# Low parts of h times W2 by seven products of quarter blocks, and PSUM emptied after each half of a tile

## What is computed

```
n  = layernorm(x)
uv = n @ in_proj_w + in_proj_b;  u, v = halves of uv;  v = silu(v)
v  = depthwise conv of 3 taps over time + conv_b
h_t = sigmoid(logit_a) * h_(t-1) + ssm_b * v_t;  y_t = ssm_c * h_t + ssm_d * v_t
a  = layernorm((u * silu(y)) @ out_proj_w + out_proj_b + n) * ln_w + ln_b
x1 = x + layernorm(a)
h  = gelu(layernorm(x1) @ T(W1) + b1)         (512 -> 2048)
x2 = x1 + layernorm(h @ T(W2) + b2)           (2048 -> 512)
```

## Time and profile before

| | us |
|---|---|
| Median of three runs | 1427.58 |
| Lowest and highest of them | 1425.25 and 1428.63 |
| The profiled execution, its own time | 1427.88 |
| Its span, first to last instruction | 1425.9 |
| DVE busy in the span | 1119.8 |
| ACT busy in the span | 911.8 |
| One tile period in the middle | 86.65 |

### The profile page before, as it was taken

One profiled execution on the slowest core, in us unless ns is written; L12 is line 12 of the kernel. 1 busy time (PEld: TensorE's weight loads), 2 busy tenths in 40 slices (PEclk: granted clock), 3 DMA queues, 4 the chain that ended last, 5 costly groups with the idle time before them and its releaser, 6 DMA issues.

```text
span 1425.9 us, 23101 instructions
## 1 busy us (share of the span) xinstructions
PE 1403.4 (98%) x8426; PEld 825.4 (58%) x8426; DVE 1119.8 (79%) x1889; ACT 911.8 (64%) x1504; POOL 414.2 (29%) x522
## 2 busy tenths in 40 slices
PE   6999999999999999999999999999999999999998
PEld 4444556656566564666646566565665646655664
DVE  8999987878779686786868778687786867998744
ACT  7998675657666565675656757476665756753553
POOL 5234241322413232142421413224132321422211
PEclk9999999999999999999999999999999999999999
DMA  8703320311311122111311203113121221001200
GB/s 248 257 27 85 65 78 17 86 30 31 89 30 60 31 53 67 31 60 31 89 31 31 74 17 89 31 30 89 23 67 30 53 67 31 31 1 30 60 30 30
DMA packets 156001, 82.26 MB, mean 58 GB/s; under 512 B 132720, under 2 KB 132720, under 8 KB 155760
## 3 DMA queue, kind: packets, MB, share of 16 engines
q1 hardware_dynamic: 155888, 80.79, 22.4%
HBM read 31.49 MB, written 16.78 MB: 34 GB/s over the span
## 4 chain that ended last, share of the span: by engine, by line
PE 86%; DVE 4%; issue 2%; DMA 0%; ACT 0%; POOL 0%; POOLq 0%; DVEq 0%; ACTq 0%
PE f1b L573 14%; PE f1b L574 14%; PE f2b L597 14%; PE f2b L599 14%; PE misc L538 6%; PE misc L536 6%; PE misc L537 6%; PE misc L550 3%; PE misc L552 3%; PE misc L551 3%; PE f2b L622 1%; PE f2b L621 1%; DVE w L1234 0%; DVE g_lo L949 0%; DMA xs<-x_dram 0%
## 5 line engine op out<-in xcount | busy, mean ns | idle before, releaser
L573 PE MATMUL f1b<-x3T,w 128*128 128x256 f16 x1792 | 397.5, 273 | 0.0
L574 PE MATMUL f1b<-x3T,w 128*128 128x256 f16 x1792 | 397.5, 273 | 0.0
L597 PE MATMUL f2b<-w,ring 128*128 128x512 fp8e5 x960 | 363.9, 379 | 0.8 <-DVE ring L847 0.8
L599 PE MATMUL f2b<-w,ring 128*128 128x512 fp8e5 x960 | 363.8, 379 | 0.0
L1652 ACT ACTIVATE ring<-f1b,par 128x256 f32<-128x256 f32 x480 | 201.2, 471 | 227.0 <-PE f1b L574 226.7
L2088 POOL TENSOR_SCALAR ve<-mv 128x4 f32<-128x4 f32 (+2 forms) x89 | 35.2, 395 | 729.8 <-DVE mv L839 729.7
L847 DVE SCALAR_TENSOR_TENSOR ring<-ring,f_sc 128x512 f16<-128x512 f32 x256 | 200.4, 796 | 30.1 <-ACT ring L1666 30.0
L574 PEld LDWEIGHTS f1b<-x3T,w 128*128 128x128 fp8e5 x1792 | 175.4, 98 | 32.6
L573 PEld LDWEIGHTS f1b<-x3T,w 128*128 128x128 fp8e5 x1792 | 175.3, 98 | 32.5
L1666 ACT ACTIVATE ring<-ring,f_sc 128x512 f16<-128x512 f32 x256 | 182.0, 718 | 0.0
L536 PE MATMUL misc<-x1T,win_hi 128*128 128x512 f16 x456 | 172.8, 379 | 0.0
(11 more groups left out here) (233 smaller groups left out, 2143.4 us busy)
## 6 DMA issues: line engine op xcount, KB each, us to landing
out_dram<-hb SPq DMA_DIRECT2D x64, 256.0 KB, 2.0
xs<-x_dram SPq DMA_DIRECT2D x14, 1024.0 KB, 6.0
ring<-w1t_dram SPq DMA_DIRECT2D x3, 1024.0 KB, 13.5
stage<-w2t_dram SPq DMA_DIRECT2D x3, 1024.0 KB, 8.2
x1T<-tp SPq DMA_TRANSPOSE x68, 3.1
xs<-x_dram SPq DMA_DIRECT2D x4, 256.0 KB, 3.6
stage<-w_in_dram SPq DMA_DIRECT2D x4, 256.0 KB, 5.0
xs<-x_dram SPq DMA_DIRECT2D x2, 512.0 KB, 6.6
```

The costliest lines, as they stand in the source:

```text
L573: pe.matmul(o_, w, src[:, k, h * TH:(h + 1) * TH], start=k == 0, stop=False)
L574: mm = pe.matmul(o_, w, src[:, KC + k, h * TH:(h + 1) * TH], start=False, stop=k == KC - 1)
L597: pe.matmul(f2b[q][:, :], h_hi[:, i % H_SLOTS, qs], w2[:, chunk, :], start=chunk == 0, stop=False)
L599: mm = pe.matmul(f2b[q][:, :], h_lo[:, i % H_SLOTS, qs], w2[:, chunk, :], start=False, stop=chunk == FC - 1)
```

## The change

**Products.** In tiles 2 to 13 (`seven(t)`) a unit's low parts, two blocks of rows by two chunks, meet W2, two chunks by two halves of its 512 columns, as a product of 2 x 2 blocks in Strassen's way: seven products of 256 columns in place of four of 512. Three of them take h_lo as it is (a11, a12, a22) and four take the sums `s1` to `s4`; four take combinations of W2 (`combined`), which DVE makes once, in step 3, in eight operations (`combine`). The high parts stay as they were.

**Sums.** The sums are made by `presums` for two units at once: four DVE operations on 16-bit values, 128 x 2 x 128, placed behind the lo of every odd unit. `presum` and `combined` lie in `stage`.

**PSUM.** The seven products need all four banks f2b in each half of a tile: f2b0 and f2b1 take the high parts and a part of the products, f2b2 and f2b3 quarter sums. So they are emptied twice: `drain(t, h)` is four operations of 256 columns, one sum of two blocks, and two operations of 512 columns. drain(t, 0) stands between the h_adds, drain(t, 1) at the head of the next step in place of the f_adds. The first half's result has a buffer in stage (`hb_first`). f2(t, 8) now waits for drain(t, 0), and PE does it behind f1(12) instead of ahead of o; f2(t, 0) waits for the whole of drain(t - 1, 1).

**Left taps.** From tile 3 on the left taps of tile s stand at the end of step s, behind the last t_lo, rather than in step s + 1.

The diff, cut to its core:

```
+    def seven(t):
+
+        return 1 < t < NT - 2
...
 
+            def f2_seven(t, j):
+
+                i, (h, chunks) = FC * t + j, unit(j)
+                p, r = chunks[0], i % H_SLOTS
+                if p == 0:
+                    pe.wait_ge(f_ok, NB * t + 2 * h)
+                if not seven(t - 1) and j == 0:
+                    pe.wait_ge(comb_ok, 8)
+                pe.wait_ge(hh_ok, i + 1)
+                for q in range(2):
+                    for n, chunk in enumerate(chunks):
+                        pe.matmul(f2b[q][:, :], h_hi[:, r, n * TH + q * P:n * TH + (q + 1) * P], w2[:, chunk, :],
+                                  start=p == 0 and n == 0, stop=False, skip_group_check=True)
+                pe.wait_ge(sums_ok, 4 * rank(i) + 4)
+                a11, a21, a12, a22 = (h_lo[:, r, n * P:(n + 1) * P] for n in range(4))
+                s1, s2, s3, s4 = (presum[:, i % 4, n, :] for n in range(4))
+                t1, t2, t3, t4 = (combined[:, n, p, :] for n in range(4))
+                left, right = slice(0, TH), slice(TH, 2 * TH)
+
+                def product(bank_, cols, a, b, start=False):
+
+                    return pe.matmul(bank_[:, cols], a, b, start=start, stop=p == PAIRS - 1, skip_group_check=True)
+
+                product(f2b[2], left, a11, w2[:, p, left], p == 0)
+                product(f2b[0], left, a12, w2[:, p + PAIRS, left])
+                product(f2b[3], right, s1, t1, p == 0)
+                product(f2b[2], right, s2, t2)
+                product(f2b[3], left, s3, t3)
+                product(f2b[0], right, s4, w2[:, p + PAIRS, right])
+                product(f2b[1], left, a22, t4).then_inc(f2_mm, 1)
+
             def f2(t, j):
+                if seven(t):
+                    f2_seven(t, j)
+                    return
                 i = FC * t + j
                 if j % PAIRS == 0 and t > 0:
-                    pe.wait_ge(f_ok, NB * (t - 1) + 2 + 2 * (j // PAIRS))
+                    pe.wait_ge(f_ok, NB * t if seven(t - 1) else NB * (t - 1) + 2 + 2 * (j // PAIRS))
...
-                left = [lambda j=j: f2(fa, j) for j in range(half(s) - LAG, half(s))] if fa is not None and s < NT else []
+                mid = min(half(s), PAIRS) if seven(fa or 0) else half(s)
+                left = [lambda j=j: f2(fa, j) for j in range(half(s) - LAG, mid)] if fa is not None and s < NT else []
...
-                        if j >= half(s) + LAG:
+                        if j >= mid + LAG:
...
+            def combine(q, g):
...
+                ve_.tensor_tensor(combined[:, q, ps, :], in0, in1, ALU.subtract, saturate=False).then_inc(comb_ok, 1)
...
+            def presums(t, j, last):
+
+                i = FC * t + j
+                r, z, k = i % H_SLOTS, i % 4, 4 * rank(i)
+                a11, a21, a12, a22 = (h_lo[:, r:r + 2, n * P:(n + 1) * P] for n in range(4))
+                s1, s2, s3, s4 = (presum[:, z:z + 2, n, :] for n in range(4))
+                if last:
+                    ve_.wait_ge(sums_ok, k + 3)
+                    ve_.tensor_tensor(s4, a12, s2, ALU.subtract).then_inc(sums_ok, 1)
+                    return
+                ve_.wait_ge(hl_ok, i + 2)
+                ve_.wait_ge(f2_mm, i - 2)
+                ve_.tensor_tensor(s3, a11, a21, ALU.subtract).then_inc(sums_ok, 1)
+                ve_.tensor_tensor(s1, a21, a22, ALU.add).then_inc(sums_ok, 1)
+                ve_.wait_ge(sums_ok, k + 1)
+                ve_.tensor_tensor(s2, a22, s3, ALU.subtract).then_inc(sums_ok, 1)
+
+            def lows(t, js, at):
+
+                items = [(at[j], lambda j=j: lo(t, j)) for j in js]
+                if seven(t):
+                    pairs = [j for j in js if j % 2 == 1]
+                    items += [(at[j] + AT_PRESUM, lambda j=j: presums(t, j - 1, False)) for j in pairs]
+                    items += [(at[j] + AT_PRESUM_LAST, lambda j=j: presums(t, j - 1, True)) for j in pairs]
+                return items
+
+            def drain(t, h):
+
+                dst, k = fo_pair(t, h), 5 * (2 * (t - 2) + h)
+                quarter = dst.rearrange("p j (n c) -> p (j n) c", c=TH)
+                left, right = slice(0, TH), slice(TH, 2 * TH)
+
+                def part(src, cols, out_, in1):
+
+                    ve_.scalar_tensor_tensor(out=out_, in0=src[:, cols], scalar=f_inv[:, 0:1], in1=in1,
+                                             op0=ALU.mult, op1=ALU.add).then_inc(part_ok, 1)
+                def first():
+                    ve_.wait_ge(f2_mm, half_done(t, h))
...
+                    part(f2b[2], left, quarter[:, 0, :], b2_row[:, 0:TH])
+                def second():
+                    part(f2b[3], right, quarter[:, 3, :], b2_step[:, :])
...
+                    part(f2b[2], right, quarter[:, 1, :], quarter[:, 0, :])
...
+                    part(f2b[3], left, quarter[:, 2, :], quarter[:, 1, :])
...
+                    ve_.tensor_tensor(dst[:, :, right], quarter[:, 1:3, :],
...
+                def block_(q):
+                    ve_.wait_ge(part_ok, k + 5)
+                    ve_.scalar_tensor_tensor(out=dst[:, q, :], in0=f2b[q][:, :], scalar=f_inv[:, 0:1], in1=dst[:, q, :],
+                                             op0=ALU.mult, op1=ALU.add).then_inc(f_ok, 1)
+                return [first, second, third, fourth, fifth, lambda: block_(0), lambda: block_(1)]
...
+                if seven(e):
+                    return (spread(AT_F_ADD, .1, drain(e, 1))
...
+                if s < NT - 1:
+                    items += [(at, lambda b=b: taps(s, b, True)) for b, at in enumerate(AT_TAP0_NEXT)]
```

More of the change, by code:

```diff
@@ L346, in hb_of, with fo_pair, fo @@
             return xs[:, NT % X_SLOTS] if c == NT - 1 else hb
+        def fo_pair(t, h):
+            return hb_first if seven(t) and h == 0 else hb[:, 2 * h:2 * h + 2, :]
+        def fo(t, j):
+            return fo_pair(t, j // 2)[:, j % 2, :]
         def xn_of(t, j):
@@ L1559, in _ @@
                     at_lo = AT_LO_PAIR if s == NT else AT_LO
-                    items += [(at_lo[j] if j < len(at_lo) else 1.2 + j, lambda j=j: lo(fa, j))
-                              for j in range(half(s))]
+                    items += lows(fa, range(half(s)), [at_lo[j] if j < len(at_lo) else 1.2 + j for j in range(FC)])
                 run(items)
@@ L1588, in _ @@
                 if c is not None:
+                    parts = drain(fa, 0) if seven(fa) else []
                     for j in range(NB):
                         h_add(c, j)
+                        for part in parts[2 * j:2 * j + 2]:
+                            part()
                         if s == NT - 1:
@@ L2133, in finish @@
                 pool.wait_ge(fn_ok, NB * e + j + 1)
-                pool.tensor_tensor(hb[:, j, :], hb[:, j, :], xs[:, e % X_SLOTS, j, :], ALU.add).then_inc(fin_ok, 1)
+                pool.tensor_tensor(fo(e, j), fo(e, j), xs[:, e % X_SLOTS, j, :], ALU.add).then_inc(fin_ok, 1)
             def keep_state(c, b):
```

74 lines of the change are left out of this document (61 added, 13 removed).

## The result

The changed kernel takes 1503.2 us (median of 4 runs, 1502.8 to 1506.2) against 1426.4 for the kernel before in the same session (1425.1 to 1428.6): a ratio of 1.054, 95% interval 1.052 to 1.056. It is slower by 77 us. The profiled execution took 1506.2 us, with a span of 1504.4.

The account below looks back on a forecast made before the run. PE bound the kernel before; DVE's queue would become the pace. 1427.9 us plus 9 (step 3 to 4), 51 (11 periods at 4.6 more) and 5 (step 15) gave 1493 us, range 1442 to 1532.

Parts of the forecast that it names:

- PE, removed: f2 units on PE: 1.63 us instead of 1.73, extra weight loads free, a period floor of 85.0 us.
- Drain: DVE's emptying of PSUM at the head of a step: 3.8 us, against two f_adds of 1.3 before.
- Sums: DVE's four sums for a pair of units: 1.03 us a pair, 8.2 us a tile (3.1 to 11.8).
- From the drain to gate 1: First stretch of a period: 32.2 us, 2.6 more than before, with PE standing 3.7 us at f2(4).
- From gate 1 to the next drain: Rest of a period: 59.1 us against 57.05 before, PE standing about 1 us at o(2), 0.5 at f2(8).
- The period: One tile, drain to drain: 91.3 us, 4.6 more than before, DVE's queue as the pace.
- The ends: Outside the 11 middle periods: 9 us more from gate 1 of step 3 to step 4's, 5 us in step 15.
- Sums at the plain rate: Rival on DVE's sums: each pair costs 0.44 us more, 1530 us in all; chance 0.2.
- PE as the pace: Rival: DVE's extra work fits its slack and PE stays the pace, 1411 us; chance 0.08.
- The falling clock: Rival: PE's clock falls because PE stops twice a step, 7 us more a step, about 1550 us; chance 0.03.
- DVE's share: Sign in the changed kernel's profile: DVE busy near 88% of the span.
- It can't fit: Step on DVE's room: 12.9 us more work a tile against 8.4 us of true slack and 1.6 us less period.

Follow-up runs that it names:

- e1: Changed kernel without the sums on DVE, the four products reading low parts instead (part of the W2 product left out): 1429.6 us, ratio 1.003.
- e13: e12 with the sums of units 6 and 7 behind gates 0 and 1 in steps 4 to 14: 1411.8 us, ratio 0.991.
- e11: Changed kernel with POOL's four additions of x1 cut to 8 of 512 columns in tiles 2 to 13: 1497.1 us, ratio 1.049.
- e3: Changed kernel with the left conv taps back in the next step, behind the drain: 1542.5 us, ratio 1.082.
- e6: Changed kernel with each drain cut to two operations of 512 columns, quarter sums not added in: 1502.0 us, ratio 1.054.
- e2: Changed kernel with the sums made, but no product reading or waiting for them: 1474.5 us, ratio 1.035.
- e5: Kernel before the change, with the sums of tiles 2 to 13 made on DVE and read by nobody: 1461.3 us, ratio 1.025.
- e7: Changed kernel with lo(4), lo(5) and their sums before the third scan, and lo(10), lo(11), lo(13) with sums in the norms' waits: 1464.9 us, ratio 1.028.
- e9: e7 with drain(t, 0) spread between x1's low parts, h_add(0) sooner, three W2 combinations in waits of step 3: 1447.9 us, ratio 1.016.
- e10: e9 with sums (2, 3) and lo(9) sooner, W2 combinations spread, seven products in tiles 2 to 12 only, old kernel end: 1429.4 us, ratio 1.0024.
- e12: e10 with right taps of blocks 0 and 1 ahead of the drain and lo(8) behind the gates, steps 4 to 14: 1422.0 us, ratio 0.9974.

## Why the prediction was right, and where it was not

The prediction of 1493 us was right in sign and near in size; the likeliest case was the one that came. The path of the prediction, DVE's queue as the pace and PE idle for about 6 us of a period, was right too: PE is idle for 92.10 - 86.11 = 6.0 us. DVE's added work is 12.5 us a tile, 12.9 predicted.

- **PE, removed.** Right: a unit takes 1.63 us, and the weight loads cost nothing. The floor of 85.0 us was 85.24 (PE's busy time) in e1 and 85.21 in e13.
- **Drain.** 3.8 us predicted, 635.56 - 631.69 = 3.87 measured.
- **Sums.** I took 1.03 us a pair. Each sum lasts 0.28 us and starts 0.2 after the one ahead; the four take 0.94. One wait of 0.11 that I had forgotten, of the first sum for the low part just ahead, makes it 1.05. That the two agree to 0.02 us is luck: the sums were taken too slow and a wait was missing. The Trainium skill (VectorE: DVE Perf Modes, "The perf-mode tier table") gives tensor_tensor twice the plain rate for bf16 in SBUF; with the 0.15 us that one element costs, (0.285 - 0.15) / 256 is 0.53 ns an element of fp16, half of the 1.04 of the earlier trace rows. So fp16 behaves here as the table has it for bf16.
- **From the drain to gate 1.** 32.2 us predicted, 33.35 measured. I put PE's one stop of 3.7 us at f2(4). It was 1.88 at f2(2) and 2.31 at f2(4), 4.2 in all. The misplaced term is POOL's blocks: I kept their cost as before, "since DVE's operations there are two-input ones as before". They cost as much as before, but fell on three of the four sums that f2(2) waits for (e11 shows that this stop is theirs). DVE's queue was also longer than I had added up: the sums of units 4 and 5 were ready 27.1 us after the drain's start, not 26.2. Of the 0.9 us 0.41 are idle time ahead of the fourth scan, which starts when ACT has ended its operation ahead of it, and ACT came to that late because of PE's f1 behind the stop at f2(2), as the waits and the order of its queue have it:

```profile
652.31 0.84 ACT L1826 ACTIVATE ring<-f1b,par 128x256 f32<-128x256 f32 x2 [1.36 <-PE f1b L600]
653.04 0.72 ACT L1840 ACTIVATE ring<-ring,f_sc 128x512 f16<-128x512 f32 x1
653.65 0.71 ACT L1875 ACTIVATE yb<-vl,par 128x512 f32<-128x512 f32 x1
...
654.45 1.28 DVE L1071 TENSOR_TENSOR_SCAN vl<-a_par,carry,vl 128x512 f32<-128x512 f32 x1 [0.41 <-issue]
```

- **From gate 1 to the next drain.** 59.1 predicted, 58.75 measured; the stops at o(2) and f2(8), 1 and 0.5 predicted, are 1.16 and 0.42.
- **The period.** 91.3 predicted (+4.6), 92.10 measured (+5.45). In 11 periods that is 9 us of the miss of 13.
- **The ends.** Step 3 to 4 cost 11.1 instead of 9, the end 7.5 instead of 5. Sum: 1427.9 + 11.1 + 59.8 + 7.5 = 1506.3, the profiled execution's 1506.2.
- **The rivals.** Sums at the plain rate: excluded by 0.28 us. PE as the pace: excluded for this order, not in general (below). The falling clock had 0.03; in the changed kernel it shows at 0.87 in one stretch at the start of the seven products (256 to 296 us, around a stop of 4.70), at 0.98 in the end (1309.66 to 1400) and at 1.00 in the tiles between. But e3 had it in every tile and e6 and e11 in most, e2 and e5 in two of the middle ones each. A fall there costs 1.7 us. The mechanism was real, the price of 7 us a step was not, and the chance was too low.
- **DVE's share.** I gave near 88% as a sign; it is 85%. The terms of the prediction themselves give 86% (1119.8 + 12 x 12.9 + 9.5 us of work in 1491), so the sign was added up wrongly.
- **A step that failed**, without harm to the number: "12.9 us more a tile, against 8.4 us of true slack ... It can't fit." Here I took the 11.0 us of DVE's waits for ACT and POOL as lost. In e13 DVE does 80.25 us of work in a period of 85.21, against 67.20 in 86.65, the same drains and sums, and PE never waits. Those waits stay as long when DVE comes later, as I wrote, but other work can stand in them: low parts, pieces of the drain, taps. In e13 2.7 us of the 11.0 are left (2.3 for ACT at the t_lo, 0.2 and 0.2 for POOL in the norms), beside 1.1 us of new waits for ACT at a low part and a scan. What was right is the walk along the queue, since it took the order as it was. What the change lacked was not room but a new order around it.

The expectations for e6, e7, e9, e10, e11 and e12 missed in one and the same way: I counted the microseconds taken from DVE's queue and did not ask who is next at that place. In e6 and e12 it was ACT's high part, in e7 PE at the drain, in e9 and e10 POOL's blocks, in e11 ACT at the fourth scan. (e1 missed by the stop at o(2) and the end, e3 perhaps by the clock.) For e13 I read from the trace that the gate's own inputs were there 0.9 us before it and that the sums were not wanted for more than 5 us, and it came out as expected.

## What to carry to other kernels

Work that is added to an engine with idle time costs nothing only if it can stand in that idle time. Find the stretch between two meetings of the engines in which the queue has no gap (here from the drain to gate 1), and move out of it whatever is not wanted before its end; the microseconds count there and nowhere else. Before you count a gain, look who is late next at that very place: six of twelve expectations here were off by that, and two more missed otherwise. And a part of a change that loses by itself (seven products, 77 us) can win when the order around it is made anew (14 us), so judge the two apart.
